# Layer 2 of a fused attention and Mamba kernel written out without a loop; u's operand built through two staging tiles and four DMAs

## What is computed

```python
# layer 0: attention with 4 heads over 4096 tokens, output projection, residual, layer norm
# layer 1: spatial 3x3 convolution + a spectral branch + mamba(u), added up
xs = silu(conv1d(in_proj(u)))
dt = softplus(dt_proj(x_proj(xs)))
dA = exp(dt * A)
h  = dA * h + dt * B * xs        # over 4096 tokens, 256 channels x 16 states, batch of 4
y  = sum_n(h * C) + xs * D
out = spatial + spectral + out_proj(y * silu(z))
```

## Time and profile before

| | before |
|---|---|
| runs | 6037.74 us median of 3 (6035.82 to 6040.58) |
| profiled execution | 6037.74 us, its span 6035.0 us |
| PE / DVE / ACT / POOL busy in the span | 92% / 80% / 61% / 70% |
| mean granted PE clock | 0.976 of full speed |
| DVE's busy share in the 13 of 40 slices of layer 1 | 90% or more in 12, 80% in the last |

### The profile page before, as it was taken

One profiled execution on the slowest core, in us unless ns is written; L12 is line 12 of the kernel. 1 busy time (PEld: TensorE's weight loads), 2 busy tenths in 40 slices (PEclk: granted clock), 3 DMA queues, 4 the chain that ended last, 5 costly groups with the idle time before them and its releaser, 6 DMA issues. The chain is left out here.

```text
span 6035.0 us, 91036 instructions
## 1 busy us (share of the span) xinstructions
PE 5545.1 (92%) x27184; PEld 2521.5 (42%) x27184; DVE 4842.5 (80%) x7122; ACT 3699.3 (61%) x7290; POOL 4212.8 (70%) x3213
## 2 busy tenths in 40 slices
PE   7999999999999999999999999968878888788787
PEld 3444444444444444444444444423333333333332
DVE  7777777777777777777777777559999999999998
ACT  3665666666666666666666666656666666666665
POOL 2777766676776677676667776647877778778787
PEclk8999999999999999999999999989999999999999
DMA  4011010110110101101100000035444444444444
GB/s 134 21 43 41 23 35 24 46 35 29 41 34 24 41 28 36 43 27 32 33 13 23 18 11 13 21 124 175 157 159 157 165 164 156 159 158 165 163 156 149
DMA packets 292556, 464.85 MB, mean 77 GB/s; under 512 B 72384, under 2 KB 95808, under 8 KB 290624
## 3 DMA queue, kind: packets, MB, share of 16 engines
q1 hardware_dynamic: 292064, 459.37, 23.4%
HBM read 381.41 MB, written 76.28 MB: 76 GB/s over the span
## 5 line engine op out<-in xcount | busy, mean ns | idle before, releaser
L560 POOL TENSOR_TENSOR sums<-exps 128x512 f32<-128x512 f32 x2048 | 2620.5, 1302 | 1310.9 <-ACT exps L493 1306.0
L569 DVE TENSOR_REDUCE mpart<-ps 128x1 f32<-128x512 f32 x4096 | 2541.9, 683 | 820.2 <-PE ps L369 820.1
L493 ACT ACTIVATE exps<-ps 128x512 f32<-128x512 f32 x4096 | 2127.6, 602 | 1404.4 <-PE ps L376 1404.0
L369 PE MATMUL ps<-k_st,q_ring 96*128 96x512 f32 x4096 | 1754.4, 429 | 17.5 <-DVE v_stage L606 7.9
L1235 POOL TENSOR_TENSOR hc<-hh,c_rep 128x512 f32<-128x512 f32 x1024 | 1363.3, 1339 | 438.2 <-DVE hh L1198 436.1
L376 PE MATMUL ps<-q_ring,k_st 98*128 98x512 f32 x4096 | 1620.7, 397 | 4.0 <-ACT exps L493 3.6
L1198 DVE TENSOR_TENSOR_SCAN hh<-d_a,carry,ps 128x512 f32<-128x512 f32 x1024 | 1298.1, 1270 | 1.1
L369 PEld LDWEIGHTS ps<-k_st,q_ring 96*128 96x128 f32 x4096 | 774.8, 189 | 1064.3 <-DVE mpart L569 547.6
L387 PE MATMUL ps<-exps,v_ring 128*32 128x512 f32 x8192 | 1090.8, 605 | 0.0
L376 PEld LDWEIGHTS ps<-q_ring,k_st 98*128 98x128 f32 x4096 | 778.0, 190 | 148.1 <-ACT exps L493 17.3
L1024 PE MATMUL ps<-s_u,sel_g 128*128 128x512 f32 x1024 | 586.5, 574 | 247.5 <-DVE hh L1198 246.7
(11 more groups left out here) (106 smaller groups left out, 3045.5 us busy)
## 6 DMA issues: line engine op xcount, KB each, us to landing
d_a<-dt_dram SPq DMA_DIRECT2D x1040, 256.0 KB
qk_split<-hilo SPq DMA_DIRECT2D x128, 256.0 KB, 2.3
q_ring<-qk_split SPq DMA_DIRECT2D x384, 64.0 KB, 2.0
k_st<-qk_split SPq DMA_DIRECT2D x45, 512.0 KB, 7.0
dt_dram<-dt SPq DMA_DIRECT2D x33, 512.0 KB, 2.8
za<-z_ext SPq DMA_DIRECT2D x33, 320.0 KB, 3.9
zp<-z_ext SPq DMA_DIRECT2D x32, 320.0 KB, 6.7
xc<-in_x SPq DMA_DIRECT2D x32, 256.0 KB, 2.9
```

Of the source, the lines that this page charges most:

```text
L369: nc.tensor.matmul(d_bank(("max", m, t)), q_ring[0:PARTS, m % 4, 128 * i:128 * i + 128], k_st[0:PARTS, g % 2, chunk(kc)], start=True, stop ...
L493: nc.scalar.activation(exps[:, u % 4, CH * half:CH * half + CH], a_bank(("exp", n, t)), ACT.Exp, scale=SCALE).then_inc(a_done, 1)
L560: pool.tensor_tensor(sums[:, u % 8, :], exps[:, u % 4, 0:CH], exps[:, u % 4, CH:2 * CH], ALU.add).then_inc(summed, 1)
L569: nc.vector.tensor_reduce(mpart[:, m % 2, t % 4, t // 4:t // 4 + 1], d_bank(("max", m, t)), AX.X, ALU.max).then_inc(d_done, 1)
```

## The change

Two things. First, the four loops are gone: all 32 iterations are written out on every engine, and `ge` waits on constants. Second, the way of u into `s_u`: ACT rounds all of `ux` in one instruction into a new tile `hi_u` (128x2x512) at g = 23; POOL subtracts at g = 23, behind its product of that group, into a new tile `lo_u`; SP then issues four DMAs of 256 KB, one for each quarter, into `s_u`, at t = 27 behind that step's load, in the queue that carries all loads (`place_u`). PE's `repeat_u` of g = 0 waits for the four landings (`u_placed`). DVE has no part in it any more.

```diff
-        def steps(e, prepare, emit, tail):
+        def steps(prepare, emit, tail):
             for g in range(G):
                 prepare(0, 0, g)
-            for it in range(2):
-                emit(it, it)
-            with e.Fori(1, NIT // 2) as k:
-                for r in range(2):
-                    emit(k * 2 + r, r)
+            for it in range(NIT):
+                emit(it, it % 2)
             tail()
...
+                def place_u(j, p):
+                    ge(sp, u_rep, (j - 1) * G)
+                    sp.wait_ge(hi_ready, j + 1)
+                    for part in range(2):
+                        a = slice(64 * part, 64 * part + 64)
+                        sp.dma_start(s_u[a, p, part::2, :].bitcast(F32), hi_u[a, :, :].bitcast(F32)).then_inc(u_placed, 16)
+                    sp.wait_ge(lo_ready, j + 1)
+                    for part in range(2):
+                        a, b = slice(64 * part, 64 * part + 64), slice(64 - 64 * part, 128 - 64 * part)
+                        sp.dma_start(s_u[b, p, part::2, :].bitcast(F32), lo_u[a, :, :].bitcast(F32)).then_inc(u_placed, 16)
...
+                        if t == 27:
+                            place_u(it + 1, 1 - p)
...
                 for g in range(NDA):
                     load_dt(0, 0, g)
+                place_u(0, 0)
...
                     if g == 0:
-                        pe.wait_ge(lo_ready, it * 2 + 2)
+                        pe.wait_ge(u_placed, it * 64 + 64)
...
-                    elif g in (23, 24):
+                    elif g == 23:
                         act.wait_ge(u_prod, j + 1)
-                        high(j, p, s_u, ux, g - 23)
+                        ge(act, u_placed, j * 64)
+                        nc.scalar.copy(hi_u[:, :, :], ux[:, :, :]).then_inc(hi_ready, 1)
...
-                def low(j, p, stack, src, part):
-                    a, b = slice(64 * part, 64 * part + 64), slice(64 - 64 * part, 128 - 64 * part)
-                    dve.wait_ge(hi_ready, j * 2 + part + 1)
-                    nc.vector.tensor_tensor(stack[b, p, part::2, :], src[a, :, :], stack[a, p, part::2, :].bitcast(F32), ALU.subtract
-                                            ).then_inc(lo_ready, 1)
-                def prepare(j, p, g):
-                    if g in (23, 24):
-                        low(j, p, s_u, ux, g - 23)
...
+                    elif g == 23:
+                        pool.wait_ge(hi_ready, j + 1)
+                        ge(pool, u_placed, j * 64)
+                        pool.tensor_tensor(lo_u[:, :, :], ux[:, :, :], hi_u[:, :, :].bitcast(F32), ALU.subtract).then_inc(lo_ready, 1)
```

More of the change, by code:

```diff
@@ L750, in layer1 @@
         ux = sb("ux", [128, 2, LC])
+        hi_u = sb("hi_u", [128, 2, LC], F32R)
+        lo_u = sb("lo_u", [128, 2, LC], F32R)
         xd = sb("xd", [128, LC])
@@ L815, in layer1 @@
          u_rep, da_ready, bu_ready, scanned, kept, hc_ready, y_done, y_added, gated, z_used, o_ready, o_copied,
-         o_full, o_even, o_odd, dt_stored) = [sem(x) for x in (
+         o_full, o_even, o_odd, dt_stored, u_placed) = [sem(x) for x in (
              "z_in", "zp_in", "flipped", "item", "item_read", "sp_log", "dt_sum", "u_prod",
              "hi_ready", "lo_ready", "u_rep", "da_ready", "bu_ready", "scanned", "kept", "hc_ready", "y_done",
-             "y_added", "gated", "z_used", "o_ready", "o_copied", "o_full", "o_even", "o_odd", "dt_stored")]
+             "y_added", "gated", "z_used", "o_ready", "o_copied", "o_full", "o_even", "o_odd", "dt_stored", "u_placed")]
         dt_in = [sem(f"dt_in{i}") for i in range(NDA)]
@@ L826, in ge @@
         def ge(e, s, value):
-            if not isinstance(value, int) or value > 0:
+            if value > 0:
                 e.wait_ge(s, value)
@@ L916, in _ @@
                 store(NIT - 1, 1)
+                sp.wait_ge(u_placed, 64 * (NIT + 1))
                 sp.wait_ge(o_even, 16 * (NIT // 2))
@@ L1031, in emit @@
                         prepare(it + 1, 1 - p, g)
-                        if g in (0, 4) and not (isinstance(it, int) and it == 0):
+                        if g in (0, 4) and it:
                             sum_states(it - 1, 6 + g // 4)
-                        if g in (12, 13) and not (isinstance(it, int) and it == 0):
+                        if g in (12, 13) and it:
                             out_proj(it - 1, g - 12)
@@ L1048, in tail @@
                         out_proj(NIT - 1, i)
-                steps(pe, prepare, emit, tail)
+                steps(prepare, emit, tail)
             @block.scalar
@@ L1062, in silus @@
                     nc.scalar.preload_act_table_set(LN_EXP)
-                def high(j, p, stack, src, part):
-                    a = slice(64 * part, 64 * part + 64)
-                    nc.scalar.copy(stack[a, p, part::2, :], src[a, :, :]).then_inc(hi_ready, 1)
                 def prepare(j, p, g):
@@ L1129, in emit @@
                             last_state(it, p, g - KEEP)
-                        elif not (isinstance(it, int) and it == 0):
+                        elif it:
                             last_state(it - 1, 1 - p, G + g - KEEP)
                         prepare(it + 1, 1 - p, g)
-                        if g == 16 and not (isinstance(it, int) and it == 0):
+                        if g == 16 and it:
                             output(it - 1, 1 - p)
@@ L1137, in output @@
                     act.wait_ge(o_ready, it + 1)
-                    if not (isinstance(it, int) and it < 2):
+                    if it >= 2:
                         act.wait_ge((o_even, o_odd)[p], (it - p) * 8)
@@ L1148, in _ @@
                 nc.scalar.preload_act_table_set(LN_EXP)
-                steps(act, prepare, emit, tail)
+                steps(prepare, emit, tail)
             @block.vector
             def _(dve):
-                def low(j, p, stack, src, part):
-                    a, b = slice(64 * part, 64 * part + 64), slice(64 - 64 * part, 128 - 64 * part)
-                    dve.wait_ge(hi_ready, j * 2 + part + 1)
-                    nc.vector.tensor_tensor(stack[b, p, part::2, :], src[a, :, :], stack[a, p, part::2, :].bitcast(F32), ALU.subtract
-                                            ).then_inc(lo_ready, 1)
-                def prepare(j, p, g):
-                    if g in (23, 24):
-                        low(j, p, s_u, ux, g - 23)
                 def add_skip(it, p, half):
@@ L1199, in emit @@
                                                      carry[:, it % STEPS, s * 8 + j:s * 8 + j + 1], ALU.mult, ALU.add).then_inc(scanned, 1)
-                        prepare(it + 1, 1 - p, g)
                         if g == 21:
                             add_skip(it, p, 0)
-                        if not (isinstance(it, int) and it == 0):
+                        if it:
                             if g == 5:
@@ L1211, in tail @@
                     add_row(NIT - 1, 1)
-                steps(dve, prepare, emit, tail)
+                steps(lambda j, p, g: None, emit, tail)
             @block.gpsimd
@@ L1238, in emit @@
                             gate(it, p, 0)
-                        if g == 6 and not (isinstance(it, int) and it == 0):
+                        if g == 6 and it:
                             gate(it - 1, 1 - p, 1)
@@ L1243, in tail @@
                     gate(NIT - 1, 1, 1)
-                steps(pool, prepare, emit, tail)
+                steps(prepare, emit, tail)
         clear(nc, names)
```

## The result

| | before | after |
|---|---|---|
| median | 6037.17 us (6035.82 to 6040.58, 4 runs) | 6361.9 us (6351.89 to 6366.08, 4 runs) |
| ratio, 95% interval | | 1.0535 (1.0516 to 1.0553) |
| span of the profiled execution | 6035.0 us | 6356.6 us |
| mean granted PE clock | 0.976 | 0.944 |

Slower, as forecast, but by 325 us where I had said 167, and outside the range. The groups on the page of the kernel after show both halves of the change: scan and product hardly differ (1282 and 689 ns, 1270 and 677 before), DVE has no idle time called issue, and it waits for PE's `repeat_u`, which waits for the DMA of the low part. (Columns: line, engine, operation, count, then busy us, mean ns, idle before and its releaser.)

The account below looks back on a forecast made before the run. DVE sets the pace before; afterwards the pieces' wait in SP's queue decides: period 67.75 us against 62.96, 6037.7 + 149 + 21 (start) - 3 (end) = 6204 us, 2.8% slower, range 6100 to 6270.

Parts of the forecast that it names:

- DVE's gain: On DVE, subtractions and loop turns vanish; alone it would need 58.19 us a period against 62.96, giving 5887 us.
- The turns: DVE's 3.73 us of issue ahead of the first product, once every two iterations, goes; 61.27 us a period without one.
- The subtractions' 3.08 us: DVE's two subtractions between scans of groups 23 to 25, 3.08 us an iteration, 95.5 us over 31 periods.
- No cost on ACT and POOL: ACT's single cast taken at 1.05 us, POOL's subtraction at 2.37 us, done by 5254.0; nothing on the path.
- SP's queue decides: In SP's in-order queue the pieces wait behind twelve loads of 1.30 us each, landing 22.66 us behind the burst's begin.
- rival 1: SP's queue wait doesn't bind, pieces perhaps passing on idle engines or out of turn; 5887 us, chance 0.08.
- Rival 4: The loads' lag doesn't carry over: about 2 us of the 8.26 us was only `out`'s; 31 x 2 less, chance 0.08.
- The pieces' term: The four pieces in SP's queue take 2.7 us behind the loads, at the dt store's rate of 387 GB/s.
- Rival 3: The queue binds harder, by a lagging DMA engine or pieces up to 1.3 us each; about 6265 us, chance 0.17.
- PE's restart: PE restarts at half clock after the landing: scan 0 at 3.97 us, in effect 4.6 us with repeat 2's delay.
- Rival 2: The queue binds but PE restarts without loss, scan 0 2.6 us behind the landing; about 6140 us, chance 0.12.
- Start and end of layer 1: Start: sixteen loads ahead of the first pieces, +21 us; end: subtractions gone from the last iteration, -3 us.

Follow-up runs that it names:

- x1_unroll: The kernel before with its loops written out and nothing else changed; 5989.2 us, ratio 0.992.
- x9_early: The changed kernel with the pieces issued at t = 19 in place of 27 and POOL's subtraction behind group 20 in place of 23; 5990.1 us, ratio 0.9926.
- x5_t24: The changed kernel with the four pieces issued at t = 24 in place of 27, behind nine loads in place of twelve; 6240.4 us, ratio 1.0338.
- x4_load16: The changed kernel with state ahead of channel in a group's partitions, so loads have 16 in their slowest dimension, not 8; 6146.1 us, ratio 1.0176.
- x2_wide: The changed kernel with each piece one row of 128 partitions in place of two rows of 64, same bytes and queue places; 6271.3 us, ratio 1.0386.

## Why the prediction was right and wrong, point by point

- **DVE's gain.** Right in both parts. The turns: by the prediction's rows 31 x (62.96 - 61.27) = 52 us, by the expectation of x1_unroll 31 x 1.8 = 56, measured 48.6. The subtractions' 3.08 us are gone from DVE's timeline, but nothing of it reaches the end.
- **No cost on ACT and POOL.** Right. One cast of 128 partitions takes 1048 ns, as one of 64 did, and SP never waited for `lo_ready` in the kernel after. POOL even gains something that I hadn't seen: with DVE's subtractions gone, the three products behind `ux` take 3.75 us in place of 4.72. x9_early showed how near POOL's edge is: three groups sooner, and product 23 came late.
- **SP's queue decides.** Right, with its order: rival 1 (pieces in time) fell, though one half of each piece did pass on the idle engines, and x5_t24 measured 1.27 us for each load ahead against 1.30. Rival 4 fell too: the twelfth load lands at 20.2 us in the kernel before, where the sum had 20.0.
- **The pieces' term and its overlap with the loads: wrong, and this is the step that failed.** I put in 4 x 262 / 387 = 2.7 us, from the store of dt, behind loads that go on at 202 GB/s as if the pieces weren't there. In the medians the last piece lands at 27.7 us and not 22.7. Of the 5.0 us, 4.0 are in the loads ahead: the pieces' halves on the idle engines run beside them, the sum of both stays at 171 to 188 GB/s, and the twelfth load lands at 24.0 in place of 20.0. The other 1.0 is the pieces' own: their last halves take 3.7 us behind it and not 2.7. Alone, four pieces take 4.9 us (214 GB/s, x4_load16), but one behind the other even that gives only 20.0 + 4.9 = 24.9. So what I had wrong most was the overlap, and the rate only after that.
- **Rival 3** had one part of it, "up to 1.3 us each like a load": 4 x 1.3 - 2.7 = 2.5 us a period, about 6282 us. Neither it nor any other rival had the loads slowed by the pieces.
- **PE's restart.** Rival 2 fell. From landing to scan 0 I had 3.97 us, and the rows give 4.0 (5260.3 to 5264.3). The further 0.6 us for repeat 2 wasn't seen: the store of dt follows scan 0 by 37.6 us as ever. That is -0.6 us a period.
- **Start and end of layer 1.** +21 forecast, +23 measured. The end: -3 forecast, +2 measured. DVE's last scan does come 3.1 us sooner, but I hadn't asked what the last `out` stands behind.
- **The sum.** In the iteration shown, 28.0 - 22.7 = 5.3 us more up to the landing and 0.6 less behind it give 72.5 in place of 67.75, so 31 x 4.75 = 147 us; with 2 for the start and 5 for the end that is 154 of the 158 that were missing. The rest is the 3.5 us by which the profiled execution lies below the median, and rounding.
- **The range** was built from lags that single rows hint at, and from no row of the thing itself: there was no 64-partition write into SBUF in the trace, and I took the fastest of the nearest rows as its price and nearly as its bound. The loads' own rate for the pieces would have been the nearer row, and beside it a term for what two streams in flight do to each other, for which the trace before had no row at all.

What stays open: why writes of one partition half go at 214 GB/s when the store of dt goes at 387, and how a piece slows the loads beside it. In the kernel after both together move less than the loads alone (171 against 204 GB/s at the start of layer 1); in x2_wide they move more (230 against 201), and yet the loads come late. That the pieces' source is to blame is excluded. That loads and pieces share a limit on the side of the writes would fit (204 GB/s for loads on 8 engines, 262 on 16, 188 with pieces beside them), but it isn't shown: no kernel here measured writes into SBUF alone at different spreads.

## What to carry to other kernels

A DMA that an engine waits for is priced from the queue and not from its size: count what is issued ahead of it in the same queue between the last drain and its issue, and multiply by what one of those takes when served, then ask how much lower the rate gets when both are in flight. Work taken off the bound engine is worth nothing if its result now travels behind a burst: pieces behind four loads and not twelve, with the subtraction made sooner, turned +5.3% into -0.7%, which is what the written-out loops gain by themselves. And the shape of the loads ahead counts: eight channels in the slowest dimension left half of the engines idle for as long as everybody waited.

## What the runs showed of the hardware that I had not expected

- With eight DMA engines busy on loads at 191 to 204 GB/s, pieces that brought the other eight in raised the share to 1.00, and the rate fell to 171 to 188 GB/s. Share isn't throughput.
- A copy into 64 partitions costs the same from SBUF and from DRAM (periods 72.5 and 72.4 us), and more than one of the same bytes into 128 (69.6 and 69.7).
- The same 1024 columns cost ScalarE 1.05 us for 64 and for 128 partitions.
- Three products on POOL took 4.72 us while DVE subtracted out of SBUF beside them, and 3.75 us without that.
